# Moving the second batch's projections and the last bulk load behind the first attention inputs

## The reference

```python
mod = (silu(c) @ wmod).reshape(16, 6, 1, 128); sa, ca, ga, sb, cb, gb = mod[:, 0..5]
ga, gb = sign(.) * max(|.|, 0.25)
h = layernorm(x) * (1 + ca) + sa
x = x + ga * attn(h)      # 16 heads of 8; softmax(Q K^T) V, + h, normalised over the batch
h = layernorm(x) * (1 + cb) + sb
x = x + gb * ffn(h)       # top 2 of 8 experts: silu(h w1 + b1) * (h w2 + b2) @ w3 + b3
```

## Time and profile before

| | |
|---|---|
| median of the runs | 1099.64 |
| profiled execution | 1099.41, its span 1097.5 |
| busy, TensorE matmuls / VectorE / ScalarE / GpSimd | 947.5 / 922.9 / 796.9 / 664.2 |
| first score of stage 0 | 41.31 |
| 32 maxima of stage 0 done, split of them begins | 67.45 |
| first exponential | 76.60 |

### The profile page before, as it was taken

One profiled execution on the slowest core, in us unless ns is written; L12 is line 12 of the kernel. 1 busy time (PEld: TensorE's weight loads), 2 busy tenths in 40 slices (PEclk: granted clock), 3 DMA queues, 4 the chain that ended last, 5 costly groups with the idle time before them and its releaser, 6 DMA issues. The chain is left out here.

```text
span 1097.5 us, 19321 instructions
## 1 busy us (share of the span) xinstructions
PE 947.5 (86%) x5725; PEld 360.7 (33%) x5725; DVE 922.9 (84%) x2045; ACT 796.9 (73%) x1493; POOL 664.2 (61%) x1033
## 2 busy tenths in 40 slices
PE   4699888998999999899998999888798999699970
PEld 2122222222222222222222222222125766466640
DVE  5788989999999999999999999999765677255666
ACT  2128888888888888888888888888676687477640
POOL 4843132675856768566685665634637667777772
PEclk9999999999999999999999999999879999899995
DMA  8979766856667566775656757522332454454556
GB/s 214 140 144 243 154 183 131 152 154 106 162 138 141 160 115 171 135 146 146 129 166 122 156 141 136 151 77 67 86 100 76 154 167 138 132 158 129 185 169 244
DMA packets 369047, 159.61 MB, mean 145 GB/s; under 512 B 290656, under 2 KB 333552, under 8 KB 365232
## 3 DMA queue, kind: packets, MB, share of 16 engines
q1 hardware_dynamic: 347376, 122.06, 50.3%
q10 hardware_dynamic: 12480, 17.57, 5.0%
q0 software_dynamic: 9088, 18.76, 4.9%
HBM read 87.85 MB, written 71.82 MB: 145 GB/s over the span
## 5 line engine op out<-in xcount | busy, mean ns | idle before, releaser
L1234 DVE TENSOR_REDUCE neg_max<-bank 128x1 f32<-128x512 f32 x1024 | 643.0, 680 | 34.6 <-PE bank L1998 31.8
L1773 ACT ACTIVATE probs<-bank 128x512 f32<-128x512 f32 x1024 | 544.3, 603 | 94.8 <-PE bank L2010 91.9
L1998 PE MATMUL bank<-Kt,Qt 48*128 48x512 bf16 x1024 | 339.1, 396 | 61.7 <-DVE neg_max L1234 47.3
L2010 PE MATMUL bank<-Qt,Kt 51*128 51x512 bf16 x1024 | 329.9, 390 | 6.2 <-ACT probs L1773 5.9
L2023 PE MATMUL bank<-probs,Vt 128*16 128x512 f32 x2048 | 274.2, 608 | 0.0
L1998 PEld LDWEIGHTS bank<-Kt,Qt 48*128 48x128 bf16 x1024 | 73.5, 94 | 400.6 <-DVE neg_max L1234 368.4
L1125 POOL DMA_INDIRECT y_dram<-y_rows,row_in x156 | 154.2, 988 | 56.9 <-issue 44.2
L1051 POOL DMA_INDIRECT rows_dram<-rows,slot x128 | 127.1, 993 | 45.4 <-issue 30.6
L1901 ACT ACTIVATE probs<-bank,w3b_cur 128x512 f32<-128x512 f32 x78 | 53.6, 688 | 56.2 <-PE bank L2048 56.1
L1659 DVE SCALAR_TENSOR_TENSOR probs<-bank,w3b_cur,probs 128x512 f32<-128x512 f32 x78 | 58.3, 748 | 38.4 <-ACT probs L1901 38.2
L2010 PEld LDWEIGHTS bank<-Qt,Kt 51*128 51x128 bf16 x1024 | 73.7, 93 | 35.8 <-ACT probs L1773 31.4
(11 more groups left out here) (236 smaller groups left out, 1210.4 us busy)
## 6 DMA issues: line engine op xcount, KB each, us to landing
o_dram<-o_sb ACTq DMA_DIRECT2D x64, 256.0 KB, 2.8
row_in<-rows_dram SPq DMA_DIRECT2D x39, 260.0 KB, 2.8
Qt<-q_dram SPq DMA_DIRECT2D x64, 128.0 KB
Kt<-k_dram SPq DMA_DIRECT2D x64, 128.0 KB
y_in<-y_dram SPq DMA_DIRECT2D x16, 512.0 KB, 4.8
q_dram<-q_parts SPq DMA_DIRECT2D x48, 128.0 KB, 4.9
k_dram<-k_parts SPq DMA_DIRECT2D x48, 128.0 KB, 5.6
rows_dram<-rows SPq DMA_DIRECT2D x4, 1040.0 KB, 5.5
```

Source lines behind the costliest of these rows:

```text
L1234: dve.tensor_reduce(neg_max[:, side, a, col:col + 1], score_a[m % 3][:], AX_X, ALU.max, negate=True).then_inc(s_max, 1)
L1773: act.activation(probs[:, 4 * (j % 2) + (k ^ 1)], score_b[n % 3][:], ACT.Exp).then_inc(s_exp, 1)
L1998: pe.matmul(score_a[m % 3][:], Qt[b % BUFS][first:first + ROWS, n, P * c:P * c + P], Kt[b % BUFS][first:first + ROWS, n], start=True, stop ...
L2010: pe.matmul(score_b[m % 3][:], Kt[b % BUFS][first:first + ROWS + PARTS, n, P * c:P * c + P], Qt[b % BUFS][first:first + ROWS + PARTS, n], ...
```

## The change

- `misc_uses`, `misc_table`: x_turn, q, k, v of batch 1 become fills of stage 0, at rounds 0, 1, 2, 3; those of batch 2 go to rounds 5, 6, 7, 10. The opening projects batch 0 only.
- SyncE: three bulk loads at first; the fourth goes behind Q's loads of batch 0. x_in for batch 1 is loaded first, then each part of q and k is stored as soon as its own step of the split is done; hT's store follows them.
- K's loads of batch 0 are issued from ScalarE's queue.
- VectorE: each batch has its own slot of `x_stats`. The opening takes statistics of batches 0 to 11; 12 to 15 come at rounds 2 to 5 of stage 0. `front_sum` for batches 3 to 15 goes; GpSimd combines the half statistics in `x_halves` in stage 0, followed by `x_power(3, NB)`. `front_shift(3, NB)` goes from round 8 to 9.
- ScalarE normalises batch 2 ahead of round 4 of stage 0.
- GpSimd: splits of batch 1's q and k move into stage 0, and `set_ones` of the third Kt behind `x_rows(3)`.

```diff
 misc_uses:
-        uses += [(q, what, 2, 0) for q, what in zip((1, 2, 4, 6), FRONT)]
+        uses += [(q, what, 1, 0) for q, what in zip((0, 1, 2, 3), FRONT)]
+        uses += [(q, what, 2, 0) for q, what in zip((5, 6, 7, 10), FRONT)]
...
 sync:
-            for i in range(4):
...
+            for i in range(3):
+                first_load(i)
...
                 if b >= BUFS:
                     sp.wait_ge(s_b, (b - BUFS + 1) * STEPS)
                 elif b:
-                    sp.wait_ge(s_x_mv, NB * TT)
+                    sp.wait_ge(s_x_stats, (8 * b - 4) * TT)
...
+            x_load(1)
+            for i in range(PARTS):
+                sp.wait_ge(s_split_q[(0, 2, 3)[i]], 1)
+                sp.dma_start(q_dram[0, i].rearrange("d n g s -> g d n s"),
+                             q_parts[:, i].rearrange("c (n s) -> c n s", s=TOK)).then_inc(s_q_stored, DMA)
+            for i in range(PARTS):
+                sp.wait_ge(s_split_k[(0, 2, 3)[i]], 1)
+                sp.dma_start(k_dram[0, i].rearrange("d n g s -> g d n s"),
+                             k_parts[:, i].rearrange("c (n s) -> c n s", s=TOK)).then_inc(s_k_stored, DMA)
             front_store(0, "x_turn")
-            x_load(1)
-            front_store(0, "q")
-            front_store(0, "k")
             q_load(0)
-            k_load(0)
+            first_load(3)
             front_store(0, "v")
+            v_load(0)
             x_load(2)
             front_store(1, "x_turn")
-            v_load(0)
...
 gpsimd:
+            def x_halves(first):
+                at = slice(TT * first, NB * TT)
+                even, odd = (x_stats[:, first:NB, :, 3 * k:3 * k + 3].rearrange("p b t c -> p (b t) c") for k in range(2))
+                pool.wait_ge(s_x_stats, NB * TT)
+                pool.tensor_tensor(x_mv[:, at, 0], even[:, :, 1], odd[:, :, 1], ALU.add)
+                pool.tensor_tensor(x_apart[:], even[:, :, 1], odd[:, :, 1], ALU.subtract)
+                pool.tensor_tensor(x_inner[:], even[:, :, 2], odd[:, :, 2], ALU.add)
...
+                pool.tensor_scalar(x_mv[:, at, 0], x_mv[:, at, 0], 0.5, None, ALU.mult)
+                pool.tensor_tensor(x_apart[:], x_apart[:], x_apart[:], ALU.mult)
+                pool.tensor_scalar(x_inner[:], x_inner[:], 1.0 / D, EPS, ALU.mult, ALU.add)
...
+                pool.tensor_scalar(x_apart[:], x_apart[:], 0.25, None, ALU.mult)
+                pool.tensor_tensor(x_ve[:, at], x_inner[:], x_apart[:], ALU.add)
...
 gpsimd, stage:
+                if b == 0:
+                    split_q(1)
+                    split_k(1)
                 if has(b, 0, NB - 1):
                     relay_v(b, par)
...
+                if b == 0:
+                    x_halves(3)
+                    x_power(3, NB)
                 if has(b, 0, NB - 1):
                     split_max(b, 0)
                 if b == 0:
                     x_rows(3)
+                    pool.wait_ge(s_x_norm, 4 * TT)
+                    set_ones(pool, 2, s_clear_odd)
+                    pool.wait_ge(s_clear_odd, 4)
...
 vector, stage:
-                if b == 0 and (r, h) == (8, 0):
+                if b == 0 and r in (2, 3, 4, 5) and h == 0:
+                    front_stats(NB - 6 + r)
+                if b == 0 and (r, h) == (9, 0):
                     front_shift(3, NB)
...
 vector, opening:
-            for b in range(4, NB):
+            for b in range(4, NB - 4):
                 front_stats(b)
-                front_sum(b - 1)
-            front_sum(NB - 1)
-            front_variance(3, NB)
...
 scalar:
+                    if r == 4 and b == 0:
+                        front_norm(2, range(TT))
...
             front_norm(1, range(TT))
-            for what in FRONT:
-                evacuate(what, 1)
-            front_norm(2, range(TT))
+            k_load()
```

More of the change, by code:

```diff
@@ L90, in misc_table @@
 def misc_table():
-    order = [(what, f, 0) for f in range(2) for what in FRONT]
+    order = [(what, 0, 0) for what in FRONT]
     for b in range(NB + 1):
@@ L173, in build @@
         probs = sb("probs", [P, 8, S])
-        x_stats = sb("x_stats", [P, 2, TT, 6])
+        x_stats = sb("x_stats", [P, NB, TT, 6])
+        x_apart = sb("x_apart", [P, (NB - 3) * TT])
+        x_inner = sb("x_inner", [P, (NB - 3) * TT])
         x_mv = sb("x_mv", [P, NB * TT, 2])
@@ L337, in build @@
         s_x_mv = sem("s_x_mv")
+        s_x_halves = sem("s_x_halves")
         s_x_ve = sem("s_x_ve")
@@ L505, in _, with first_load @@
                 sp.dma_start(dst, src).then_inc(s_w, DMA)
-            for i in range(4):
+            def first_load(i):
                 low = 1 if i == 0 else 0
@@ L883, in x_power @@
                 pool.tensor_tensor(x_rstd[:, at], x_ve[:, at], neg_half[:, at], ALU.pow).then_inc(s_x_rstd, 1)
+            def x_halves(first):
+                at = slice(TT * first, NB * TT)
+                even, odd = (x_stats[:, first:NB, :, 3 * k:3 * k + 3].rearrange("p b t c -> p (b t) c") for k in range(2))
+                pool.wait_ge(s_x_stats, NB * TT)
+                pool.tensor_tensor(x_mv[:, at, 0], even[:, :, 1], odd[:, :, 1], ALU.add).then_inc(s_x_halves, 1)
+                pool.tensor_tensor(x_apart[:], even[:, :, 1], odd[:, :, 1], ALU.subtract).then_inc(s_x_halves, 1)
+                pool.tensor_tensor(x_inner[:], even[:, :, 2], odd[:, :, 2], ALU.add).then_inc(s_x_halves, 1)
+                pool.wait_ge(s_x_halves, 3)
+                pool.tensor_scalar(x_mv[:, at, 0], x_mv[:, at, 0], 0.5, None, ALU.mult).then_inc(s_x_mv, (NB - first) * TT)
+                pool.tensor_tensor(x_apart[:], x_apart[:], x_apart[:], ALU.mult).then_inc(s_x_halves, 1)
+                pool.tensor_scalar(x_inner[:], x_inner[:], 1.0 / D, EPS, ALU.mult, ALU.add).then_inc(s_x_halves, 1)
+                pool.wait_ge(s_x_halves, 5)
+                pool.tensor_scalar(x_apart[:], x_apart[:], 0.25, None, ALU.mult).then_inc(s_x_halves, 1)
+                pool.wait_ge(s_x_halves, 6)
+                pool.tensor_tensor(x_ve[:, at], x_inner[:], x_apart[:], ALU.add).then_inc(s_x_ve, 1)
             def f_sums(f):
@@ L1108, in _ @@
             x_power(2, 3)
-            split_q(1)
-            split_k(1)
             pool.memset(rows[:], 0.0).then_inc(s_idle_row, 1)
@@ L1113, in _ @@
             pool.wait_ge(s_idle_row, 2)
-            pool.wait_ge(s_x_mv, NB * TT)
+            pool.wait_ge(s_x_stats, 8 * TT)
             set_ones(pool, 1, s_clear_odd)
-            set_ones(pool, 2, s_clear_odd)
-            pool.wait_ge(s_clear_odd, 4)
-            x_power(3, NB)
+            pool.wait_ge(s_clear_odd, 2)
             over_stages(pool, stage)
@@ L1201, in front_stats @@
                     dve.wait_ge(s_x_first[b // 4], DMA)
-                if b >= 2:
-                    dve.wait_ge(s_x_mv, TT * (b - 1))
                 src = x_in if b == 0 else x_first[b // 4][:, b % 4]
                 for t in range(TT):
-                    dve.bn_stats(x_stats[:, b % 2, t], src[:, t]).then_inc(s_x_stats, 1)
+                    dve.bn_stats(x_stats[:, b, t], src[:, t]).then_inc(s_x_stats, 1)
             def front_sum(b):
@@ L1210, in front_sum @@
                 for t in range(TT):
-                    dve.bn_aggr(x_mv[:, TT * b + t], x_stats[:, b % 2, t]).then_inc(s_x_mv, 1)
+                    dve.bn_aggr(x_mv[:, TT * b + t], x_stats[:, b, t]).then_inc(s_x_mv, 1)
             def front_variance(first, last):
@@ L1840, in stage, with k_load @@
                         copy_o(b - 1, (r + QUADS - LAG) // 4 - 1)
+            def k_load():
+                act.wait_ge(s_clear, 3)
+                act.wait_ge(s_k_stored, PARTS * DMA)
+                for group, i, part, count in K_SLOTS:
+                    for a in range(2):
+                        row = HALF * a + group + SPREAD * DK * i
+                        rows = slice(row, row + SPREAD * DK * count - group, SPREAD)
+                        act.dma_start(Kt[0][rows].rearrange("r n q -> r (n q)"),
+                                      k_dram[0, part:part + count, :, N8 * a:N8 * a + N8]
+                                      .rearrange("i d n g s -> (i d) (n g s)")).then_inc(s_k_landed[0], DMA)
             front_norm(0, range(TT))
@@ L2081, in _ @@
             ins.then_inc(s_mod_turn, 1)
[L2082 to L2085, removed]
+            for what in FRONT[1:]:
+                fill(what, 0)
             pe.wait_ge(s_mod_rows, 1)
```

2 lines of the change are left out of this document (removed).

## The result

The changed kernel takes 1106.61 us (median of 5 runs, 1105.86 to 1108.21) against 1099.64 (5 runs, 1098.10 to 1101.14): ratio 1.0060, 95% interval 1.0043 to 1.0077. It is 7.0 slower; forecast was 1.2 faster, with a range that ended at 1101.8. The profiled execution has a span of 1104.1, 6.6 more than before.

What follows compares the result with a forecast made beforehand. It took score matmuls and row maxima as the bound, the start being set by K's store and load. Start -6.2, fills +4.0, statistics +1.3, GpSimd +0.1, later stages -0.4 make -1.2 on 1099.41: median 1098.4, range 1094.0 to 1101.8.

Steps and rivals of the forecast that it cites:

- The term of the bulk load beside K: Opening: the fourth bulk load, moving beside K's last loads, delays the first score by 0.7 (bounds nothing and 3.6).
- at the same price in ScalarE's: Opening: K's eight loads take 4.96 to issue from ScalarE's queue, as in SyncE's, from 27.0 to 32.0.
- the sum without the bulk load: Opening: K stored near 27.0, issues 4.96, then 2.35 to the first score, at 34.4 before the bulk load's delay.
- -0.4 (between -0.7 and +0.7): Later stages: SyncE some 5 late, but expert weights move away from stage 1's maxima moves; 0.4 gained.
- a difference of over a microsecond in stage 1 or 2: Stages 1 and 2: differing from before by over a microsecond would show the forecast wrong.
- GpSimd's power fits: Stage 0: GpSimd's power ends 31.2 after the first score, in time for round 9 by 0.1; 0.1 charged.
- Stage 0 as a whole: Stage 0 grows by fills +4.0, exposed statistics +1.3 and GpSimd's 0.1.
- The clock rises sooner: Stage 0: fills bring TensorE to its upper clock before round 12, so later fills shorten; 1094.4, chance 0.22.
- K's loads are dear in ScalarE's queue: Opening: K's issues take 8.5 instead of 5.0, first score 38.6 to 39.6; 1102.4, chance 0.12.
- The second queue saves nothing: Opening: K's bytes come no sooner than behind Q's, first score 37.7; 1101.0, chance 0.04.
- The start gains more: Opening: bulk load doesn't meet K's loads, stores go out faster by parts, first score 33.6; near 1096.9, chance 0.09.
- GpSimd is late at round 9: Stage 0: slow strided operations or a late bulk load make TensorE and VectorE wait for the power; 1101.7, chance 0.07.

Runs made afterwards that it cites:

- a1: Changed kernel, but SyncE issues the fourth bulk load only after K's loads land, with v's store and load of batch 0 ahead of it; 1103.15 us, ratio 1.0047.
- d2: c3 with GpSimd's copy of batch 2's v moved behind the split of the maxima in stage 2's first half; 1099.57 us, ratio 1.0000.
- c3: a1 with SyncE's load of v for batch 2 and store of v for batch 3 moved behind the load of batch 0's reciprocals; 1103.48 us, ratio 1.0042.
- d1: c1 with GpSimd's copy of batch 2's v moved behind the split of the maxima in stage 2's first half; 1104.16 us, ratio 1.0049.
- b1: Changed kernel, but in stage 2 GpSimd splits the maxima ahead of batch 4's k; 1104.44 us, ratio 1.0043.
- b4: Kernel before, with five memsets of an unused tile on GpSimd ahead of stage 2's first split of the maxima; 1101.31 us, ratio 1.0021.
- a3: Changed kernel, but GpSimd sets the third Kt buffer's ones behind batch 2's splits; 1104.43 us, ratio 1.0055.
- a2: Changed kernel, but K's loads go back to SyncE's queue, behind Q's and ahead of the fourth bulk load; 1106.07 us, ratio 1.0066.
- c1: Changed kernel, with SyncE's load of v for batch 2 and store of v for batch 3 behind the load of batch 0's reciprocals; 1106.12 us, ratio 1.0060.
- b3: Changed kernel rebuilt: batch 1's x_turn, q, k filled in the opening, batch 2's at rounds 2 to 5, bulk load after K, GpSimd reordered; 1094.70 us, ratio 0.9955.
- a4: a1 with GpSimd setting the third Kt buffer's ones behind batch 2's splits; 1099.97 us, ratio 1.0011.

## Why the prediction was wrong

**Wrong, the largest: "I take 0.7, since only K's last two or three loads meet it, and these queues share rather than follow each other".** The term of the bulk load beside K was mis-sized: it measures 2.9 between the profiles of after and a1 and 3.8 over five profiles each, which is its own upper bound of 3.6 and not 0.7. The argument looked at when the loads are issued. What counts is whether their bytes are still to be moved: in 34:36 the DMA engines were full, all of K's issues were out, and the first score needed the last of them. From the last issue of K to the first score it took 6.6 with the bulk load and 3.3 without it (a1). To share the engines with it was no cheaper for K than to come behind it.

**Wrong, smaller, in the same sum.** K's issues taken "at the same price in ScalarE's" queue: 5.76, and 5.68 to 6.25 over all runs, instead of 4.96. From the end of the issues to the first score: 2.35 forecast, 3.3 in a1, without the bulk load. Stores done at 27.5 instead of 27.0. With these three (27.6 + 6.0 + 3.3) the first score of a1 is 36.99 where the sum without the bulk load said 34.4. The start was worth 4.4 at best, not 6.2, against a stage 0 that is 4.9 longer: the change as drawn could not gain, and d2, in which both faults are mended, measures 1.0000.

**Wrong: later stages "-0.4 (between -0.7 and +0.7)".** This step looked at when SyncE's entries of stage 1 are due and at the maxima's moves, not at what stands behind them in the same queue. SyncE, by the forecast some 5 late, was 8.5 late from batch 2's stores on (3.4 of the stage, 3.65 of `set_ones`, the rest waits for x_in), had made good only 2.2 of it when the reciprocals' load came, and four things hang on that load in a row: `add_h`, y's statistics on VectorE, the split of the maxima, TensorE. Behind TensorE's wait of 2.66 the granted clock then read 0.50 for 3.4. Shown by d2 against a1 and c3 (chain mended, times clear of each other), by d1's profile (loss 0.2) and by b1 (one waiter moved away, the next one waits); b4 (split late in the kernel before, loss 1.0) points the same way, within what profiles differ by. How the 2.3 divides between the wait and the lower clock no run separates: a3 lost 1.7 behind a wait of 1.40 at a clock of 1.00. The prediction had named a difference of over a microsecond in stage 1 or 2 as a sign of being wrong, but none of its cases led there.

**Right.** The stores' new place in the queue brings K's landing forward (27.5 against 27.0 forecast, and an estimated 31.4 before); no run tells that place apart from the storing by parts. Fills: 1.45 of VectorE's idle time each, 0.68 where statistics stand before them. Statistics hidden at rounds 2 and 3. The combining's operations at 52 columns 0.24 to 0.38 (0.28 forecast). GpSimd's power fits, with nothing to spare: it ended 30.9 after the first score, forecast 31.2; the split behind it is 1.5 later than the maxima allowed, for which TensorE waited 0.30 and VectorE not at all. Stage 0 as a whole +4.9 against +5.4.

**The rivals.** *The clock rises sooner* did not happen: the fills of stage 0 still took 2.07. *K's loads are dear in ScalarE's queue* names the side and the first score (38.6 to 39.6, measured 39.90), but neither the time (1102.4 against 1106.61) nor the mechanism: the issues took 5.76, not 8.5. Its first score came out by luck. *The second queue saves nothing* is refuted as put (a1 against a2: 1.4). *The start gains more* and *GpSimd is late at round 9* did not occur. No case had stage 2.

**Open.** Why the clock fell behind a wait of 1.84 in c3's profile and not behind the same 1.84 in c1's or 1.80 in b4's, when c3's own executions fall into two kinds; and why it stayed low for 3.4 in two profiles and some 10 in three. Also where the last 0.5 between the 32nd mark and the end of the changed kernel's profile comes from; it is of the size by which profiles differ.

## What to carry to other kernels

A bulk transfer that nobody needs yet is put behind the landing of the loads that the start waits for, not behind their issue, and its own first reader is looked up too (in b3 VectorE then waited 1.76 for it); look at the DMA share of the stretch into which it will fall. For an engine or queue that a change makes late, walk down its whole program to the first entry whose consumer has no slack, and count what is behind it on every engine in turn. When a wait is taken away, name the next consumer of the same late result: in b1 it was that one which waited. In c1 the edit itself had put a new wait into the chain.

## What was not expected of the hardware

- Behind a wait of TensorE of 2.06 to 2.68 in stage 2 the granted clock read 0.50, for 3.4 (after, b1) or some 10 (a1, a2); behind 1.24, 1.40 and 1.80 it did not (a4, a3, b4), and behind 1.84 it did in one profile (c3, some 10) and not in another (c1). With a wait of 2.68 stage 2 lost 6.2 (a1), more than twice that length, of which 1.9 was made good by the end of the span.
- One kernel can have both kinds of execution: c3's twelve are 1100.39 to 1101.25 at a mean granted clock of 0.972, or 1103.28 to 1108.57 at 0.966 to 0.969. Its median alone does not show that.
- A version with an earlier start can lose more in stage 2 than a later one: a1 lost 6.2 there, after 2.3, with the same wait.
- K's eight loads of the opening took 4.96 to issue from SyncE's queue (before, a2) and 5.68 to 6.25 from ScalarE's (twelve profiles), where SyncE's queue was issuing at the same time.
- The first score varies by 1.6 between profiles while the bulk load shares the engines with K (39.90 to 41.51), and by 0.3 where it waits (36.73 to 36.99).
